# Two graph-attention layers on one NeuronCore: all twelve attention heads turned by DMA, four heads with the maximum as the exponent's offset, ELU's minimum on VectorE, and a new order of the pieces

## What is computed

```python
# layer 0: 6 heads of 64
q, k, v = heads(x @ Wq + bq), heads(x @ Wk + bk), heads(x @ Wv + bv)
probs = softmax(q @ k.T / 8 + where(adj, 0, -9e15))
x = layernorm(x + (probs @ v) @ Wf + bf)
# layer 1: 12 heads of 32
h = einsum('bnd,ade->bane', x, W); th = tanh(h)
a = leaky_relu(th @ w_src + (th @ w_dst).T, 0.2)
a = softmax(where(adj, a, -999))
f = elu(a @ h + b)
g = sigmoid(x @ H_w.T + H_b)
x = layernorm(x + g * f + (1 - g) * x)
```

## Time and profile before

| | |
|---|---|
| median of 3 runs | 1208.75 us |
| the profiled execution's own time | 1210.46 us |
| its span, first to last instruction | 1208.7 us |
| busy: TensorE, VectorE, ScalarE, GpSimd | 1104.2, 1000.4, 978.8, 938.4 us |
| mean granted clock of TensorE | 0.977 of full speed |
| DMA, mean share of 16 engines | 25.2% |
| layer 1's last pass, heads turned on TensorE (L621) | 256 transposes, 41.4 us |

### The profile page before, as it was taken

One profiled execution on the slowest core, in us unless ns is written; L12 is line 12 of the kernel. 1 busy time (PEld: TensorE's weight loads), 2 busy tenths in 40 slices (PEclk: granted clock), 3 DMA queues, 4 the chain that ended last, 5 costly groups with the idle time before them and its releaser, 6 DMA issues.

```text
span 1208.7 us, 36231 instructions
## 1 busy us (share of the span) xinstructions
PE 1104.2 (91%) x12490; PEld 1002.8 (83%) x12553; DVE 1000.4 (83%) x2012; ACT 978.8 (81%) x1932; POOL 938.4 (78%) x813
## 2 busy tenths in 40 slices
PE   3699999999999999999999999999999999999953
PEld 3689988888998888899888889988888998888842
DVE  4568988888898888889888888988888898888864
ACT  4358888888888888888888888888888888888864
POOL 1137888888888888888888888888888888888786
PEclk9899999999999999999999999999999999999985
DMA  4013332112332211233221123332112232211322
GB/s 158 15 30 66 64 78 67 48 39 77 77 76 77 67 47 40 77 77 76 77 67 49 38 77 77 76 77 67 50 37 77 77 76 77 67 50 38 78 51 61
DMA packets 179226, 78.40 MB, mean 65 GB/s; under 512 B 157813, under 2 KB 174202, under 8 KB 179194
## 3 DMA queue, kind: packets, MB, share of 16 engines
q1 hardware_dynamic: 179194, 77.98, 25.2%
HBM read 31.22 MB, written 12.58 MB: 36 GB/s over the span
## 4 chain that ended last, share of the span: by engine, by line
PE 78%; DVE 9%; POOL 5%; issue 5%; DMA 2%; ACT 1%; SPq 1%; POOLq 0%; ACTq 0%; DVEq 0%
PE lin L453 45%; PE zp L550 6%; PE fp L635 5%; DVE z L1124 4%; PE zp L608 3%; PE zp L612 3%; PE fp L638 3%; DVE ctx_n L1083 3%; PE fp L575 3%; PE tp L560 3%; PE tp L621 2%; PE fp L578 2%; PE tp L492 2%; PE lin L497 1%; PE tp L587 1%
## 5 line engine op out<-in xcount | busy, mean ns | idle before, releaser
L1329 POOL TENSOR_TENSOR z<-z,z_max 128x1536 f32<-128x1536 f32 x64 | 176.4, 2756 | 47.8 <-DVE z_max L1131 47.8
L1341 POOL TENSOR_TENSOR f<-f,x_kept 128x384 f32<-128x384 f32 x64 | 64.8, 1012 | 109.6 <-DVE f L1156 109.6
L1336 POOL TENSOR_TENSOR p_lo<-z,p_hi 128x1024 f16<-128x1024 f32 x64 | 137.8, 2154 | 1.4 <-ACT p_hi L833 0.7
L1288 POOL TENSOR_TENSOR prod<-th,w_sd_rows 128x768 f32<-128x768 f32 x64 | 119.9, 1874 | 6.4 <-ACT th L738 6.2
L802 ACT ACTIVATE z<-zp 128x1536 f32<-128x1536 f32 x64 | 93.1, 1454 | 34.7 <-PE zp L612 34.6
L793 ACT ACTIVATE p<-p,p_min 128x128 f32<-128x128 f32 x384 | 119.4, 409 | 0.0
L1124 DVE SCALAR_TENSOR_TENSOR z<-zp,z 128x1536 f32<-128x1536 f32 x64 | 112.1, 1752 | 5.2 <-ACT z L802 5.2
L1131 DVE TENSOR_REDUCE z_max<-z 128x12 f32<-128x1536 f32 x64 | 111.9, 1748 | 0.1
L635 PE MATMUL fp<-h_part,p1t_hi 128*128 128x33 bf16 x2304 | 105.1, 178 | 2.4 <-DVE p1t_lo L1137 1.3
L453 PE MATMUL lin<-xt_hi,Wq_hi 128*128 128x256 f32 x288 | 88.0, 306 | 19.9 <-POOL xt_lo L1312 13.4
L635 PEld LDWEIGHTS fp<-h_part,p1t_hi 128*128 128x128 f16 x2304 | 101.0, 96 | 5.7 <-issue 1.8
(11 more groups left out here) (165 smaller groups left out, 4520.0 us busy)
## 6 DMA issues: line engine op xcount, KB each, us to landing
xt_raw<-x_t SPq DMA_DIRECT2D x32, 384.0 KB, 3.2
x_raw<-x SPq DMA_DIRECT2D x32, 384.0 KB, 3.2
out<-out_tile SPq DMA_DIRECT2D x64, 192.0 KB, 2.4
adj<-adj SPq DMA_DIRECT2D x64, 32.0 KB, 2.5
dst_row<-sd_t SPq DMA_DIRECT2D x64, 9.0 KB
p1t_hi<-p_hi SPq DMA_TRANSPOSE x64, 2.8
p1t_lo<-p_lo SPq DMA_TRANSPOSE x64, 2.8
z<-Wq SPq DMA_DIRECT2D x1, 576.0 KB, 3.5
```

The lines of the kernel that those rows point to most:

```text
L1288: pool.tensor_tensor(prod[:, g, :].rearrange("p (s d) -> p s d", s=2), th[:, g:g + 1, :].to_broadcast([128, 2, D]), rows["w_sd"][:, :].rea ...
L1329: pool.tensor_tensor(zs, zs, z_max[:, g, :].unsqueeze(2).to_broadcast([128, H1, N]), ALU.subtract)\
L1336: pool.tensor_tensor(p1_lo[:, g, :], z[:, g, PE_HEADS * N:], p1_hi[:, g, :], ALU.subtract).then_inc(w1_lo[g].sem, 1)
```

## The change

Six things change.

- `weights1_transposes`, `turned1_high` and `turned1_low` are gone. `weights1_high` and `weights1_low` now split all twelve heads (128 x 1536 instead of 128 x 1024), and both DMA transposes take 1536 columns.
- `z_subtract` handles heads 0 to 7 only. VectorE's new `z_shift` makes log(16384) minus the maximum, and `z_exponent` becomes four exponentials of 128 columns with that as offset, then one of 1024 columns.
- `features_negative` moves from ScalarE (Relu of 1 - f) to VectorE (min of f and 1); `elu_exp` takes the offset -1 instead of the scale -1.
- `attend1(g, 0)` now waits for both DMA transposes.
- SyncE, TensorE, ScalarE, VectorE and GpSimd all have new lists, and the banks new owners.
- The tiles `p1_hi` and `p1_lo` grow to twelve heads.

```diff
-LIN_USERS = ("h1", "qk0", "g0", "pr0", "g1", "pr1", "v0", "qk1", "qk2", "v1", "h0")
+LIN_USERS = ("qk0", "pr0", "pr1", "g1", "v0", "qk1", "qk2", "v1", "h0", "h1", "g0")
-TP_USERS = ("pt01", "pt00", "pt11", "sdt", "pt10", "ct0", "ct1", "x1t0", "wt0", "wt1", "x1t1")
+TP_USERS = ("pt11", "pt10", "ct0", "ct1", "x1t0", "x1t1", "pt00", "pt01", "sdt")
-FP_USERS = ("f1", "ctx0", "ctx1", "f0")
+FP_USERS = ("ctx0", "ctx1", "f0", "f1")
+SECOND_BANK = ("pr0", "pr1", "v0", "qk2", "h0", "g0", "pt11", "ct1", "x1t0", "sdt")
...
-                    sp.dma_start_transpose(p1t_lo[:, g, PE_HEADS * N:].rearrange("p (a n) -> p a n", a=DMA_HEADS),
-                                           p1_lo[:, g, :])\
+                    sp.dma_start_transpose(p1t_lo[:, g, :].rearrange("p (a n) -> p a n", a=H1), p1_lo[:, g, :])\
...
                     if k == 0:
                         bank_free(FP_USERS, f"f{g}")
                         pe.wait_ge(h_done[2][g].sem, prev(h_done[2][g]))
-                        pe.wait_ge(wt_lo[g].sem, now(wt_lo[g]))
-                    if k == 1:
                         pe.wait_ge(wt_turned[g].sem, prev(wt_turned[g]))
...
                 def z_exponent(g):
+                    act.wait_ge(z_offsets[g].sem, now(z_offsets[g]))
+                    for h in range(SUBTRACTED, H1):
+                        act.activation(z[:, g, N * h:N * (h + 1)], z[:, g, N * h:N * (h + 1)], ACT.Exp,
+                                       bias=z_offset[:, g, h:h + 1])
                     act.wait_ge(z_sub[g].sem, now(z_sub[g]))
-                    act.activation(z[:, g, :], z[:, g, :], ACT.Exp, bias=log_scale[:, :]).then_inc(z_exp[g].sem, 1)
+                    act.activation(z[:, g, 0:SUBTRACTED * N], z[:, g, 0:SUBTRACTED * N], ACT.Exp, bias=log_scale[:, :])\
+                        .then_inc(z_exp[g].sem, 1)
...
+                def z_shift(g):
+                    dve.wait_ge(z_maxed[g].sem, now(z_maxed[g]))
+                    dve.wait_ge(z_exp[g].sem, prev(z_exp[g]))
+                    dve.tensor_scalar(z_offset[:, g, :], z_max[:, g, :], -1.0, math.log(PSCALE), ALU.mult, ALU.add)\
+                        .then_inc(z_offsets[g].sem, 1)
...
+                def features_negative(g):
+                    dve.wait_ge(f_norm[g].sem, now(f_norm[g]))
+                    dve.wait_ge(f_elu[g].sem, prev(f_elu[g]))
+                    dve.tensor_scalar(f_neg[:, g, :], f[:, g, :], 1.0, None, ALU.min).then_inc(f_min[g].sem, 1)
```

More of the change, by code:

```diff
@@ L26 @@
 PSCALE = 16384.0
[L27 removed]
 WEIGHTS = ("Wq", "Wk", "Wv", "Wf", "W1", "Hw")
 DONE_BY_DMA = 16
+SUBTRACTED = 8
 SMALL = 5
@@ L675, in body @@
                 turn.step(2, attend1, 0, 0)
+                turn.step(1, hidden, 1)
+                turn.step(0, weights0_transposes, 0, 0)
                 turn.step(2, attend1, 0, 1)
+                turn.step(2, attend1, 0, 2)
+                turn.step(1, gate_rows, 0)
+                turn.step(0, weights0_transposes, 0, 1)
+                turn.step(2, attend1, 1, 0)
+                turn.step(2, attend1, 1, 1)
+                turn.step(1, source_target_transposes)
             turns(pe, passed, body)
@@ L882, in body @@
[L882 to L888 removed]
+                turn.late(1, z_exponent, 0)
+                turn.late(1, weights1_high, 0)
+                turn.late(1, gate_tanh, 1)
+                turn.step(0, value_part1, 0)
@@ L915, in body @@
-                turn.step(1, gate_tanh, 0)
+                turn.late(2, norm1, 0)
+                turn.step(0, scores_exp, 0)
+                turn.step(1, hidden_tanh, 1)
+                turn.step(0, weights0_high, 0, 0)
+                turn.late(2, norm1, 1)
+                turn.step(1, hidden_part1, 0)
+                turn.step(0, scores_exp, 1)
+                turn.step(0, value_part2, 1)
+                turn.step(0, weights0_high, 0, 1)
+                turn.step(1, source_target_copy)
@@ L1178, in shift_norm1 @@
                         .then_inc(norm1_shift[g].sem, 1)
+                turn.late(0, scores_masked, 0)
+                turn.late(0, scores_min, 0)
+                turn.late(0, value_residue, 1)
+                turn.late(1, x1_low, 1)
+                turn.late(0, scores_masked, 1)
+                turn.late(0, scores_min, 1)
+                turn.late(1, source_target_sums, 0)
+                turn.late(1, hidden_raised, 0)
+                turn.late(0, weights0_low, 0, 0)
+                turn.late(2, features_inverse, 0)
+                turn.late(2, features_norm, 0)
+                turn.late(1, source_target_sums, 1)
+                turn.late(1, source_target_part1)
+                turn.late(1, source_target_residue)
+                turn.late(1, source_target_part2)
+                turn.late(2, features_negative, 0)
+                turn.late(1, source_target_part3)
+                turn.late(1, hidden_raised, 1)
+                turn.late(0, weights0_low, 0, 1)
+                turn.late(2, features_inverse, 1)
+                turn.late(2, features_norm, 1)
+                turn.late(2, elu, 0)
+                turn.late(2, features_negative, 1)
                 turn.late(0, weights0_low, 1, 0)
-                turn.late(0, context_low, 0)
-                turn.late(2, elu, 1)
+                turn.late(0, context_inverse, 0)
+                turn.late(0, context_norm, 0)
+                turn.late(0, weights0_low, 1, 1)
                 turn.late(0, context_inverse, 1)
@@ L1185, in body @@
                 turn.late(1, z_leak, 0)
-                turn.step(0, queries_keys, 0)
-                turn.late(0, add_residual, 0)
-                turn.late(0, context_low, 1)
-                turn.late(0, stats0, 0)
-                turn.late(0, moments0, 0)
-                turn.late(0, variance0, 0)
-                turn.late(1, z_maxima, 0)
-                turn.late(0, shift_norm0, 0)
+                turn.late(0, context_low, 0)
+                turn.late(1, z_maxima, 0)
+                turn.late(2, elu, 1)
+                turn.late(1, z_shift, 0)
+                turn.late(0, context_low, 1)
+                turn.late(0, add_residual, 0)
+                turn.step(0, queries_keys, 0)
                 turn.late(1, z_leak, 1)
```

210 lines of the change are left out of this document (69 added, 141 removed).

## The result

The changed kernel takes **1298.75 us** (median of 4 runs, 1297.48 to 1300.42), the kernel before 1209.13 beside it (4 runs): ratio 1.0742, 95% interval 1.0723 to 1.0760. It is slower by 90 us. The forecast was 1199 with a range up to 1255; what happened lies near the far end (1305) of the second rival.

A forecast was written before the change was run, and what follows sets the result against it. TensorE's list and uncovered round trips bound the kernel; 32.9 us work plus 1.97 waits made a 34.87 us turn, 0.35 less. Over 32 turns: 1210.46 - 11.2 + 2 = 1201.3 for the profiled execution, so 1199; range 1180 to 1255.

The forecast's parts named there:

- the second rival: The minima on VectorE wait for GpSimd as well: 1226 or 1257 us, up to 1305; chance 0.22.
- What bounds the kernel: Before the change: TensorE's own work, 33.8 us of a 35.22 us turn, and round trips that it can't cover.
- The costs engine by engine: Per-engine gains and losses: TensorE loses 0.9 us a turn, GpSimd net +0.3, ScalarE about zero, VectorE -0.13 a graph.
- (d): TensorE from hidden(1)'s end to source_target_transposes: 5.09 us of chain against 4.45 of work, so a wait of 0.64.
- (c): project(1) follows project(0) in one bank, which add_residual(0) must read between: 0.8 us of uncovered wait.
- (b): attend0(0) takes the bank of f1, which features_norm(1) reads: 0.25 us more wait.
- (a): weights0_transposes(1, 1) takes the bank that source_target_copy reads: 0.28 us of wait.
- Where the order is tight: VectorE's four tiny pieces and minimum stand beside GpSimd's second v_part; part3 would wait 0.4 us more.
- Both readings: GpSimd's lock holds up only two-input VectorE instructions (turn below 35.3 us), or the new minima too (35.7 or more).
- the cluster: VectorE's tiny pieces and minimum beside GpSimd's v_part: part3 0.8 us late, or 1.8 if h_res goes between.
- the nearer ends: Within the second rival, prices nearer 1226 us than 1305 were called likelier.
- The DMA's landing: Transposes land in about 4.2 us instead of 2.8, hidden before attend1(1, 0); late landing, 1233 us, had chance 0.05.

The follow-up runs named there:

- the other form: The changed kernel with gaps in f_neg's tile, so VectorE's minimum writes in three runs of 128 columns: 1287.8 us.
- the first run: The changed kernel with two waits added on GpSimd: value_part3(1) for source_target_part3, next_x_low for the minimum of graph 1: 1216.91 us, ratio 1.0052.
- the fourth kernel: The changed kernel with one wait added on GpSimd: next_x_low waits for the minimum of graph 1: 1286.1 us.

## Why the prediction was wrong, point by point

- **What bounds the kernel**: TensorE's list and the round trips that it can't cover. Right as far as the runs go: in the turns that are taken apart above, what the turn gained or lost stands in TensorE's waits or in its clock.
- **The costs engine by engine** held: landing 3.7 to 3.8 for 4.2, subtraction 1.90 for 1.84, low part 3.14 for 3.23, the minimum undisturbed 0.35 for 0.36, z_shift 0.17 for 0.19, and the exponential of 1024 columns 1.15 for 1.1. The choice for the minimum, by the cast's pace, was right, and the upper end (0.55) is what the other form measured.
- **Terms (a) to (d)**: (d) 5.18 for 5.09 once the lock is cleared. (c): `project(1)` starts 2.79 behind `project(0)`, a piece of 1.73, so 1.06 for 0.8. (b): `attend0(0)` starts 1.08 behind the six transposes, of 0.65, so 0.43 for 0.25. (a): the transposes come 0.95 behind `source_target_transposes`, forecast 0.86 + 0.05; the time is right and its cause wrong, since `attend1` itself starts 0.45 after them, where the work is 0.3, and no wait is left for the copy. Together the turn was put 0.53 too short, 17 us: nearly all between the first run's 1217 and 1199.
- **Where the order is tight** is the step that failed. It had v_part ready at 4.35 after `hidden(1)` (its terms add up to 4.37) against part2 at 4.43. The trace has 4.37 (569.91 - 565.54) and 4.45: right within 0.02 us. Then it chose the reading in which only an instruction with two inputs waits, and with it a wait of 0.4 for part3 alone; the sum that gave 1199 had not even that in it. The runs show that the fast one-input instructions wait as well: part2 0.86 for 0.19, the second minimum 1.97 for 0.35, and with both cleared 82 of the 90 us are gone. Both readings were on the page, and the row that speaks for the other one was there as well: a cast at double pace. The second rival had 0.22; the evidence at hand bore more.
- **The second rival's price**: the cluster was put at 0.8 or 1.8 late and took 1.34 (6.43 for 5.09), since the cast waits too and h_res goes between, though VectorE's own piece passes first. The second minimum was put at 1.5 and cost 1.35 by the turns. Its far end of 1305 was 6 us off, in part by luck: the cluster had been put too dear at 1.8, while the sum under it was 17 us short and the clock's 10 us were in no case. The range stopped at 1255 on the words that the nearer ends are likelier, and nothing in the rows said so: by the new lists both places meet GpSimd in every turn, so if the minimum takes the lock at all, both are paid for.
- **The granted clock** was in no case. It took 10 us here and 32 in the fourth kernel, each time behind a standstill that the lock had made.
- **The DMA's landing** was hidden, as forecast; TensorE's waits for it (14.1 us, two of them) lie outside the steady turns.

The Trainium skill (SBUF — State Buffer, on SBUF's two separate sides) states the lock for two SBUF inputs or a mode that uses both ports, held for a whole instruction, and the trace agrees: with GpSimd beside it the minimum takes 1.97 in the fast form and 0.545 in the form of three runs, which does not wait at all. By the Trainium skill's page VectorE: DVE Perf Modes (the perf-mode tier table) the minimum would run in such a mode; its 0.35 against 0.545, and its wait, agree.

## What to carry to other kernels

Before moving a piece to VectorE, look in the new order for what GpSimd does at that moment, and count a fast-form or two-input piece at the remaining length of GpSimd's instruction; if a rule and a row both allow it, give it the larger chance. A wait removed counts only if the next reader in line is early: walk down the line, with the reader's own engine, before pricing it. And do not read "busy" as work: VectorE was busy for 65 us more than before, and 79 us went when nothing collided.
